# A DLRM tower on one core: twelve resident tables looked up instead of eleven, and gathers held back by a new signal from within the slot products

## What is computed

```python
e = jnp.stack([tbl_0[ids[:, 0]], ..., tbl_25[ids[:, 25]]], axis=1)      # 512 x 26 x 128
combined = jnp.concatenate((dense[:, None, :], e), axis=1)              # 512 x 27 x 128
inter = jnp.einsum('bfd,bgd->bfg', combined, combined)[:, iu, ju]       # pairs f < g
h = jnp.concatenate([dense, inter, dense], axis=1)                      # 607 columns
h = jnp.maximum(h @ W_top1 + b_top1, 0.0)                               # 512
h = jnp.maximum(h @ W_top2 + b_top2, 0.0)                               # 256
y = h @ W_top3
```

## Time and profile before

| | |
|---|---|
| runs | 124.36, 124.73, 125.06 us |
| profiled execution, first to last instruction | 123.0 us |
| end of the lookups on PE | 52.8 us |
| start of passes 1 to 4 on PE | 53.7, 74.9, 92.8, 110.1 us |
| busy: PE, DVE, ACT, POOL | 104.2, 65.4, 48.1, 65.7 us |
| transferred | 13.51 MB |

### The profile page before, as it was taken

How to read it: one execution, slowest core, us unless ns; L and a number is a source line. 1 busy time by engine, 2 the same in 40 slices (tenths; PEclk the granted TensorE clock), 3 DMA queues, 4 the chain that set the end, 5 groups by cost and what they waited for, 6 DMA issues and landing times.

```text
span 123.0 us, 3436 instructions
## 1 busy us (share of the span) xinstructions
PE 104.2 (85%) x1516; PEld 87.9 (71%) x1516; DVE 65.4 (53%) x110; ACT 48.1 (39%) x81; POOL 65.7 (53%) x66
## 2 busy tenths in 40 slices
PE   6999999999999999962178996289995299998993
PEld 6787888888888888831067895177992278996991
DVE  2599999999899996820001742105540106451411
ACT  4542979197794931300000462002541102730321
POOL 3887888579878887877500887503778305000000
PEclk9999999999999999999555999756999558999999
DMA  3799999999211112121200111200112100000000
GB/s 57 236 400 365 402 398 408 410 392 368 80 43 45 45 43 48 44 63 43 64 5 5 43 43 43 64 0 0 45 43 64 43 0 20 23 0 0 0 0 1
DMA packets 3949, 13.51 MB, mean 110 GB/s; under 512 B 1315, under 2 KB 1317, under 8 KB 3302
## 3 DMA queue, kind: packets, MB, share of 16 engines
q1 hardware_dynamic: 2018, 9.48, 20.5%
q0 software_dynamic: 1920, 3.94, 11.2%
q10 hardware_dynamic: 4, 0.00, 0.0%
HBM read 13.42 MB, written 0.00 MB: 109 GB/s over the span
## 4 chain that ended last, share of the span: by engine, by line
PE 83%; issue 13%; DVE 2%; ACT 1%
PE bank L365 17%; PE prod L408 13%; PE bank L414 13%; PE prod L365 12%; PE bank L374 7%; PE bank L504 6%; PE prod L433 4%; PE bank L321 4%; PE bank L325 3%; PE bank L445 2%; DVE inter_s L585 1%; PE bank L438 1%; PE prod L421 1%; PE bank L421 0%; DVE xT L575 0%
## 5 line engine op out<-in xcount | busy, mean ns | idle before, releaser
L313 POOL DMA_INDIRECT emb<-in_tbl,ids_sb x60 | 65.0, 1083 | 38.3 <-PE prod L408 19.3
L522 DVE TENSOR_SCALAR mask<-ids_h,ids_sb 128x1024 fp32r<-128x1024 int16 (+1 forms) x48 | 31.5, 699 | 2.2 <-issue 0.8
L408 PE MATMUL prod<-xT 128*27 128x27 f32 x1024 | 16.8, 215 | 14.7 <-issue 14.2
L408 PEld LDWEIGHTS prod<-xT 128*27 128x27 f32 x1024 | 13.6, 128 | 18.8 <-issue 17.4
L585 DVE STREAM_TRANSPOSE inter_s<-prod 128x288 f32<-128x288 f32 (+1 forms) x8 | 4.6, 611 | 26.3 <-PE prod L408 26.3
L365 PE MATMUL bank<-mask,high 128*128 128x512 f32 x46 | 15.2, 393 | 0.0
L365 PE MATMUL bank<-mask,low 128*128 128x512 f32 x46 | 15.0, 390 | 0.0
L414 PE MATMUL bank<-pairs,w_sb 117*128 117x128 f32 x96 | 12.7, 282 | 0.1
L414 PEld LDWEIGHTS bank<-pairs,w_sb 117*128 117x128 f32 x96 | 11.6, 191 | 0.7 <-ACT pairs L696 0.5
L531 DVE TENSOR_TENSOR low<-table,high 128x1024 fp32r<-128x1024 f32 (+1 forms) x9 | 11.7, 1301 | 0.0
L374 PE MATMUL bank<-ident,emb 128*128 128x128 f32 x60 | 10.5, 310 | 0.9 <-issue 0.9
(11 more groups left out here) (55 smaller groups left out, 118.1 us busy)
## 6 DMA issues: line engine op xcount, KB each, us to landing
table<-in_resident SPq DMA_DIRECT2D x3, 1024.0 KB
w_sb<-in_weights SPq DMA_DIRECT2D x1, 1792.0 KB
table<-in_resident SPq DMA_DIRECT2D x1, 1280.0 KB
table<-in_resident SPq DMA_DIRECT2D x4, 256.0 KB
emb<-in_tbl,ids_sb POOLq DMA_INDIRECT x60
ids_h<-in_other_ids SPq DMA_DIRECT2D x1, 896.0 KB
table<-in_resident SPq DMA_DIRECT2D x1, 640.0 KB
ids_h<-in_pair_ids SPq DMA_DIRECT2D x1, 256.0 KB
```

The source lines that it names most:

```text
L313: nc.gpsimd.indirect_dma_start(out=rows(t, c), out_offset=None, in_=gathered[c], in_offset=bass.IndirectOffsetOnAxis(ap=ids_sb[:, i:i + 1] ...
L408: mm = nc.tensor.matmul(prod[SLOT_PITCH * q:SLOT_PITCH * q + SLOTS, i, 0:SLOTS], x, x, start=True, stop=True)
L522: nc.vector.tensor_scalar(made(step)[:, 0:n, :], ids_h[:, 2 * b:2 * b + n, :], col_sb[:, row:row + 1], None, ALU.is_equal).then_inc(s_mask, 1)
```

## The change

One more table is resident, so that the last lookup is a pair too, in the bank `y_bank` and in `t_bank[1]`, which holds transposed groups otherwise. There are 14 gathers a tile, 56 in all, and groups 2 and 3 have three tables each. The waits on `s_used` (the last), `s_prod` and `s_l1` in `hold` are replaced by waits on a new semaphore, `s_quiet`, that PE raises after 16 of the 64 matmuls of the second half. Around the two banks a wait is added (`s_pack[1]`) and one is moved (`s_kept_last`), and DVE packs and keeps two looked-up tables at the end instead of one.

```diff
-RESIDENT = 11
+RESIDENT = 12
 GATHERED = TABLES - RESIDENT
...
-GROUPS = [(0, 4), (4, 4), (8, 4), (12, 3)]
+GROUPS = [(0, 4), (4, 4), (8, 3), (11, 3)]
...
+STIR = MATMULS // 2 + 4
...
-        look_banks = [l1_bank, half_bank, l1_bank, half_bank, l1_bank, [y_bank]]
+        look_banks = [l1_bank, half_bank, l1_bank, half_bank, l1_bank, [y_bank, t_bank[1]]]
...
+        s_quiet = sem("s_quiet")
...
                 if (t, i) == (2, 0):
                     pool.wait_ge(s_used, first_step[4] + 3)
-                if (t, i) == (2, 6):
-                    pool.wait_ge(s_used, first_step[5] + 3)
-                if (t, i) == (2, 10):
-                    pool.wait_ge(s_prod, 1)
-                if (t, i) == (3, 0):
-                    pool.wait_ge(s_l1, 2)
-                if (t, i) == (3, 4):
-                    pool.wait_ge(s_prod, 2)
-                if (t, i) == (3, 9):
-                    pool.wait_ge(s_l1, 4)
-                if (t, i) == (3, 13):
-                    pool.wait_ge(s_prod, 3)
+                if (t, i) == (2, 8):
+                    pool.wait_ge(s_quiet, 1)
+                if (t, i) == (3, 1):
+                    pool.wait_ge(s_quiet, 2)
+                if (t, i) == (3, 8):
+                    pool.wait_ge(s_quiet, 3)
...
+                if b == len(PAIRS) - 1:
+
+                    pe.wait_ge(s_pack[1], 1)
                 look_up(b)
...
-                products(range(MATMULS // 2, MATMULS)).then_inc(s_prod, 1)
+                products(range(MATMULS // 2, STIR)).then_inc(s_quiet, 1)
+                products(range(STIR, MATMULS)).then_inc(s_prod, 1)
...
                     dense_part(samples, (0, 1))
+                pe.wait_ge(s_kept_last, 1)
                 turn_next(p, (1,))
 
-                pe.wait_ge(s_kept_last, 1)
                 pe.wait_ge(s_y, p)
...
             dve.wait_ge(s_used, first_step[-1])
+            nc.vector.tensor_copy(*pack_looked(RESIDENT - 2))
             nc.vector.tensor_copy(*pack_looked(RESIDENT - 1)).then_inc(s_ready, 1)
+            nc.vector.tensor_copy(*keep_looked(RESIDENT - 2))
             nc.vector.tensor_copy(*keep_looked(RESIDENT - 1)).then_inc(s_kept_last, 1)
...
-                        dve.wait_ge(s_known, RESIDENT - 1)
+                        dve.wait_ge(s_known, RESIDENT - 2)
```

## The result

The change made the kernel slower. In the comparison on record it took 131.94 us (median of 4 runs) against 124.9 for the kernel before; the ratio is 1.052, interval 1.038 to 1.066. The forecast was 113.0. Two of the four runs took 130.6 us and two, in a slower state that any kernel here falls into at times, 133.2 and 134.2; the profile is of one of the former.

What follows compares the result with a forecast made beforehand. PE, idle or crawling through products while gathers fly, was taken as the bound. Pass starts 58.3, 70.0, 82.5, 97.4 plus 12.9 gave 110.3; 1.0 for the clock made 111.3, 1.7 from span to median 113.0 us; range 108.5 to 119.

Steps and rivals of the forecast that it cites:

- What bounds: Products in passes 1 to 3: some 4 records per gather while gathers fly; PE idle 14.7 us ahead of them.
- The lookup: Last pair ahead of pass 1: 20 more matmuls, +4.55 us, DVE keeping up at 0; products start at 58.3.
- The failed step: Pass 2 products: 4.8 us in all, first half +1.6, second half an undisturbed 1.27 despite the gathers starting.
- the first rival: Second halves of passes 1 to 3: products crawl once a gather starts, not its transfer; 135 us, chance 10%.
- the rest of each pass behind the products: From products' end to the next pass: 7.7 us in passes 1 and 2, nearly as before.
- The crawl of 1.9 us into the next first halves: Passes 2 and 3: last gathers release 1.9 us into the products; first half 2.9 instead of 1.27, +1.6 each.
- The wait in pass 3: Ahead of group 3's transposes: PE idles 2.4 us for tile 3's last gather, held by the third signal.
- 1.0 for the clock: Pass 3's wait: allowance for products and layer two at half clock, taken between bounds 0 and 2.6 us.
- The second rival: PE's loop in the passes: stalls come from code loading, not gathers, so passes keep their lengths; 129 us, chance 3%.
- 3.5 us of crawls: First halves of products: crawl terms of 0.3 us in pass 1 and 1.6 each in passes 2 and 3.

Runs made afterwards that it cites:

- f2: Kernel before without POOL's six waits from tile 2's seventh gather on: 133.57 us against 124.6 for the kernel before (ratio 1.077).
- r1: Changed kernel with gathers held until the end of the products, on the crawling chip: 120.17 us against 124.6 for the kernel before (ratio 0.968).
- f3: Changed kernel without its three waits on the new signal, leaving the twelfth table: 130.36 us against 124.6 for the kernel before (ratio 1.039).
- c1: The changed kernel itself, measured again on a chip without crawls: 115.15 us against 106.47 for the kernel before (ratio 1.084).
- e2: Changed kernel without the 20 gathers behind the three signals, so some rows are wrong: 108.74 us against 106.98 for the kernel before (ratio 1.020).
- e1: Changed kernel with gathers held until the end of the products, on a chip without crawls: 115.62 us against 106.98 for the kernel before (1.086).
- b1: The unchanged kernel before, run again for its profile on a chip without crawls: 105.7 us against 106.99 for the same kernel (ratio 0.990).
- u1: Changed kernel with PE's loop of four passes written out: 115.87 us against 106.99 for the kernel before (ratio 1.086).

## Why the prediction was wrong

- **What bounds.** "While gathers are in flight the products crawl" was right, for the chip of the record: f2 against its own passes 3 and 4, and r1. That the crawl is not there on every chip was not seen, and one profile could not show it.
- **The lookup.** Right: products start at 58.25, 58.3 forecast; DVE never held the last pair (its last masks are done at 53.3, PE's last matmul starts at 57.2). That is for the record; in the other runs with twelve tables the products start at 58.1 to 59.4.
- **The failed step** is in pass 2: "Products 1.27 + 1.6 + 0.25 + 0.44 + 1.27 = 4.8", with "second halves of 1.3 us right through the first gather's start". It set the gather's cost from its transfer on. The second half took 9.5 us in pass 2, crawling from 0.2 us after POOL's row begins, 1.4 us ahead of the first transfer, and the crawl of 8.6 us went on into the last gather. r1, with the signal moved to the end, gives back 12 us. This was the first rival, at 10%: "the gate opens too early", 135. It hit the place and the direction. Its price was too high because in passes 1 and 3 the products escaped, in pass 3 since POOL woke only at their end, in pass 1 behind their stop; what suffered there was the hand-over. When a gather's start is felt is thus not settled by one number: 0.2 us in pass 2, not within 0.9 us in pass 1, 1.1 us in f2.
- **The hand-over.** A second step that failed: the rest of each pass behind the products, 7.7 us, took the work between engines as untouched by gathers. In passes 1 and 3 DVE and ACT started 2.0 to 3.2 us late, the clock fell, and what is behind the products took 11.9 and 14.9 us, against 7.7 and 10.1 forecast (the 10.1 with the wait of pass 3, which did not come). In pass 2 it took 11.1. The profile of before had a sign of it, which the prediction does not mention: VectorE's and ScalarE's work after layer two waited up to 5.7 us for something "remote" while gathers and products overlapped.

```profile
97.98 0.35 DVE L611 TENSOR_SCALAR h<-bank,ids_sb 128x128 f32<-128x128 f32 x1 [5.73 <-remote]
```

- **A stop in pass 1.** The sum has nothing for the 0.68 us between records 85 and 86 of its second half. It comes at that record, at 0.3 to 1.3 us, in every run with twelve tables and the loop but f3, with or without gathers behind the signal.
- **The crawl of 1.9 us into the next first halves** did not come on record, since the passes had grown; it came in r1 (3.8 us for the half, against 2.9 forecast).
- **The wait in pass 3**, forecast 2.4 us with 1.0 for the clock, did not come on record either, for the same reason. On the other chips it came larger: 3.7 us in c1 and 1.0 of clock in layer two alone (3.09 us for 2.05).
- **The second rival**, code and not gathers, is refuted by f2 on the crawling chip: with the same loop, and no gathers left, its pass 3 takes 11.2 us. e2's 11.2 and 11.4 us were measured where nothing crawls and can't decide it.
- **The sum.** Against the forecast the start and pass 4 are within 0.1 us, passes 1 to 3 are 4.9, 10.0 and 3.5 longer, and the 1.0 for the clock is in these: 17.4 us of the 18.9 between 113.0 and 131.94. The other 1.5 is that the median lies 3.2 us above this span, not 1.7. Where nothing crawls the forecast of 113.0 would have been near (115.15), but by luck: it holds 3.5 us of crawls that are not there. The kernel before takes 106.5 there, and the change loses 8.7 us by other means: 4.5 or somewhat more for the table, about 4 for the third wait.

No version that gathers all its rows beat the kernel before on both kinds of chip. The late signal (r1) beats both kernels on the crawling one and loses on the other (e1, 1.086).

## What to carry to other kernels

A signal that lets background work start "just before the end" of a sensitive stretch rests on a guess about when that work begins to hurt, and the transfer is not a safe guess. Look in the trace for what such work does when it starts inside the stretch, and if no row shows it, put the signal at the end. When transfers are held back, add up whether what is behind the last hold still lands in time: here that wait alone cost 4 us. And before a large idle time of one profile is planned away, see whether another chip has it.

## What the runs showed of the hardware

- Small dense matmuls (10 ns a record) slow down while a gather is in flight, by 0.5 us per half of 128 records on three chips (e1, c1, b1: 1.7 to 1.8 us for 1.27), and to some 4 to 6 records per 0.72 us, or per twice that, where they crawl (77.97, 78.70, 79.43 in the profile after). Layer one, at some 9 records per us, keeps its pace under gathers in either (20 records in 2.46 us in b1 and in r1).
- The same program took 106 to 107 us on four chips and 124.6 on another; a pass without gathers takes the same on both (11.2 us in f2, 11.15 and 11.4 in e2).
- After a gather's row began the crawl set in 0.2 us later in pass 2 of the change and 1.1 us later in f2.
- With gathers just started, DVE or ACT took up PE's result 2.0 to 3.2 us late in the profile on record; in r1, on the crawling chip, the same steps were prompt.
- Behind 3.7 us of idle PE the clock fell to half, about 1 us after work had begun again (c1: layer two 3.09 us for 2.05); behind 1.70 us it stayed up (u1: layer two 1.95 us).
